# Moving a scale computation and a tile ahead in an attention and feed-forward block, and the place where its score banks change order

## What is computed

```
xn = layernorm(x)
s = attention(xn, Wq, Wk, Wv, Wo)      # 16 heads of 32, rope, causal softmax
h = gelu(bitlinear(xn, w_fc))          # 2048 hidden; ternary weights
g = silu(bitlinear(h, w_proj))
out = x + s * g
```

## Time and profile before

| | |
|---|---|
| median of 3 runs | 1154.88 us (1153.55 to 1155.67) |
| profiled execution, its own time | 1155.67 us |
| its span, first to last instruction | 1154.0 us |
| TensorE busy | 1108.0 us, 96% |
| VectorE busy | 856.8 us, 74% |
| ScalarE busy | 789.0 us, 68% |
| GpSimd busy | 506.0 us, 44% |

### The profile page before, as it was taken

How to read it: one execution, slowest core, us unless ns; L and a number is a source line. 1 busy time by engine, 2 the same in 40 slices (tenths; PEclk the granted TensorE clock), 3 DMA queues, 4 the chain that set the end, 5 groups by cost and what they waited for, 6 DMA issues and landing times.

```text
span 1154.0 us, 20237 instructions
## 1 busy us (share of the span) xinstructions
PE 1108.0 (96%) x7548; PEld 605.3 (52%) x7548; DVE 856.8 (74%) x1596; ACT 789.0 (68%) x1508; POOL 506.0 (44%) x915
## 2 busy tenths in 40 slices
PE   4989899999999999999999999999999999999997
PEld 3555654447444574446644475445844467444763
DVE  6987966788557885588756886579855888558864
ACT  4787884578835888179862788447882588727984
POOL 2035351473615626175342745146361553526433
PEclk9999999999999999999999999999999999999999
DMA  8491002730019101371016410183002910145111
GB/s 309 156 109 41 1 3 65 92 83 29 2 35 145 50 2 30 42 123 37 3 29 77 89 37 3 29 104 88 12 2 48 145 37 2 30 53 76 38 37 40
DMA packets 52610, 67.30 MB, mean 58 GB/s; under 512 B 9376, under 2 KB 34336, under 8 KB 52000
## 3 DMA queue, kind: packets, MB, share of 16 engines
q1 hardware_dynamic: 52512, 66.02, 30.0%
HBM read 31.98 MB, written 8.40 MB: 35 GB/s over the span
## 4 chain that ended last, share of the span: by engine, by line
PE 73%; DVE 7%; ACT 7%; POOL 6%; DMA 3%; issue 3%; SPq 1%; POOLq 0%; DVEq 0%; ACTq 0%
PE banks L421 20%; PE banks L547 18%; PE banks L592 11%; PE banks L526 5%; PE banks L673 4%; PE banks L438 4%; POOL arena L1374 4%; PE banks L603 3%; ACT banks L854 2%; ACT arena L877 2%; PE banks L654 2%; PE banks L533 2%; DVE mix L1142 2%; PE banks L452 1%; DMA stacks<-split_buf 1%
## 5 line engine op out<-in xcount | busy, mean ns | idle before, releaser
L854 ACT ACTIVATE banks<-banks,mix,scl 128x384 f32<-128x384 f32 (+2 forms) x384 | 248.6, 650 | 34.7 <-POOL mix L1351 32.0
L1142 DVE TENSOR_REDUCE mix<-banks 128x1 f32<-128x512 f32 (+3 forms) x352 | 215.5, 636 | 31.5 <-PE banks L533 27.3
L547 PE MATMUL banks<-xT,fcT 128*128 128x512 f16 x1024 | 227.9, 379 | 4.8 <-ACT xh_buf L818 4.7
L592 PE MATMUL banks<-proj_ones,arena 128*128 128x256 f16 (+1 forms) x1536 | 213.5, 273 | 0.3 <-DVE mix L1070 0.3
L1336 POOL TENSOR_TENSOR split_buf<-xr_buf,split_buf 128x512 f16<-128x512 f32 x64 | 74.6, 1186 | 314.2 <-ACT split_buf L795 314.2
L877 ACT ACTIVATE arena<-banks,scl 128x1280 f32<-128x1280 f32 x128 | 164.7, 1329 | 33.5 <-PE banks L654 29.3
L1342 POOL TENSOR_TENSOR xh_buf<-xh_buf 128x512 f32<-128x512 f32 x120 | 152.6, 1272 | 48.3 <-ACT xh_buf L818 42.0
L421 PE MATMUL banks<-xT,qkT 128*128 128x512 f16 x768 | 168.7, 379 | 0.0
L547 PEld LDWEIGHTS banks<-xT,fcT 128*128 128x128 f16 x1024 | 98.5, 98 | 124.3 <-ACT xh_buf L818 9.5
L592 PEld LDWEIGHTS banks<-proj_ones,arena 128*128 128x128 f16 x1536 | 141.3, 97 | 36.4 <-issue 0.6
L1351 POOL TENSOR_SCALAR mix<-mix,scl 128x1 f32<-128x1 f32 (+1 forms) x288 | 77.1, 268 | 182.2 <-DVE mix L1142 180.5
(11 more groups left out here) (163 smaller groups left out, 1469.2 us busy)
## 6 DMA issues: line engine op xcount, KB each, us to landing
stacks<-split_buf SPq DMA_DIRECT2D x192, 128.0 KB, 5.1
out_dram<-arena SPq DMA_DIRECT2D x32, 256.0 KB, 2.0
xr_buf<-in_L_attn_x_dram SPq DMA_DIRECT2D x7, 1024.0 KB, 6.9
resid<-in_L_attn_x_dram SPq DMA_DIRECT2D x28, 256.0 KB, 4.8
stacks<-in_L_ffn_w_fc_dram SPq DMA_DIRECT2D x1, 4096.0 KB, 25.9
arena<-in_L_ffn_w_proj_dram SPq DMA_DIRECT2D x1, 4096.0 KB, 14.8
mix<-norm_row SPq DMA_DIRECT2D x8, 256.0 KB, 4.9
xr_buf<-in_L_attn_x_dram SPq DMA_DIRECT2D x4, 256.0 KB, 3.8
```

The source lines that it names most:

```text
L547: mm = pe.matmul(banks[:, UP_BANKS[f % NUB], :], fcT[:, c, f * P:(f + 1) * P], xT[:, part, c, :], start=(c == 0 and part == 0), stop=(c == ...
L592: mm = pe.matmul(banks[:, DOWN_BANKS[h % 3], 0:cols.stop - cols.start], hid[:, part, f, t * P:(t + 1) * P], proj_ones[:, f, cols], start=( ...
L854: mm = nc.scalar.activation(block, block, ACT.Exp, scale=col(EXP_SCALE), bias=exp_bias[:, i, h0 + k:h0 + k + 1], accum_out=row_sum[:, i, h ...
L1142: nc.vector.tensor_reduce(row_max[:, i, h0:h0 + n], scores_of(r), AX_X, ALU.max).then_inc(max_ready, 1)
```

## The change

Four things are moved. The two rows of `S_BANKS` in which the order of banks changes stand at rounds 25 to 34 where they stood at rounds 15 to 24. VectorE scales tile 0 of the block before ahead of the up projection, after RoPE, and GpSimd adds its residual ahead of the squares' additions. VectorE makes `gate_scale` directly after centring, ahead of `finish_context(0)`. ScalarE's tanh no longer waits for `ffn_step`.

```
-S_BANKS = 3 * (3, 4, 0, 2, 1) + (3, 0, 4, 2, 1) + (0, 3, 2, 4, 1) + 4 * (0, 2, 3, 4, 1)
+S_BANKS = 5 * (3, 4, 0, 2, 1) + (3, 0, 4, 2, 1) + (0, 3, 2, 4, 1) + 2 * (0, 2, 3, 4, 1)
...
-OUT_SCALED_AFTER = 3
...
                     act.wait_ge(centred, b * NT + NT)
-                    act.wait_ge(ffn_step, b * 7 + 6)
                     nc.scalar.activation(tanh_sb[:, t, :], gate[:, t, :], ACT.Tanh,
...
+                if not first:
+                    scale_by_gate(b - 1, b * 8 + 8, range(OUT_EARLY))
+
                 def scores_of(r):
...
-                    if f == OUT_SCALED_AFTER and not first:
-                        scale_by_gate(b - 1, b * 8 + 8, range(OUT_EARLY))
...
                     centre(t, gate[:, t, :])
+                dve.wait_ge(rstd_ready, b + 1)
+                step(6, nc.vector.scalar_tensor_tensor(gate_scale[:, 0, :], rstd, col(HALF_GP), nan_if_0, ALU.mult, ALU.mult))
+                if not first:
+                    step(7, nc.vector.tensor_scalar(gate_scale[:, 1, :], gate_scale[:, 0, :], col(SVO), None, ALU.mult))
+
                 def finish_context(g):
...
-                    if g == 1:
-                        dve.wait_ge(rstd_ready, b + 1)
-                        step(6, nc.vector.scalar_tensor_tensor(gate_scale[:, 0, :], rstd, col(HALF_GP), nan_if_0, ALU.mult, ALU.mult))
-                        if not first:
-                            step(7, nc.vector.tensor_scalar(gate_scale[:, 1, :], gate_scale[:, 0, :], col(SVO), None, ALU.mult))
...
+                if not first:
+                    for t in range(OUT_EARLY):
+                        add_x(b - 1, t)
                 for f in range(1, FC):
...
-                    if f == OUT_SCALED_AFTER and not first:
-                        for t in range(OUT_EARLY):
-                            add_x(b - 1, t)
```

## The result

The changed kernel is slower: 1180.7 us median of 4 runs (1180.1 to 1181.3) against 1154.2 us for the kernel before, a ratio of 1.0228 with a 95% interval of 1.021 to 1.0246. That is 26.5 us more; 19.8 were forecast, with a range that ended at 1180. The direction, the two new stalls and the places without cost are as predicted. What took the time out of the range is a cost that the prediction did not have at all: 8.0 us in the profiled execution, some 6 in the timed ones.

The account below looks back on a forecast made before the run. TensorE, busy 96% of the span, was taken as the bound. Terms of 11.4 (early scale), 8.4 (bank order) and 0 (tile 0) sum to 19.8 us, making 1174.7 us from the 1154.88 median; range 1170 to 1180.

Parts of the forecast that it names:

- the two new stalls: TensorE waits at the heads' weighing for the context copy, 11.4 us, and in the score rounds for bank sums, 8.4 us.
- the places without cost: Tile 0's early scaling and residual add, and the tanh's dropped wait, were to cost and gain nothing.
- The bound: TensorE, busy 96% of the span; another engine's time costs nothing unless a matmul waits for it.
- Part 1, the stall: Heads' stage: early gate scale delays the context copy, so `weigh(2, 0)` starts 1.43 us late per middle block; 11.4 us in all.
- The choice of the shorter power: Masks and power on GpSimd take 1.75 us without `normalise` beside them; 11.4 us by this, 14.1 without.
- The step that failed: Behind `weigh(2, 0)` TensorE has no wait of 0.1 us or more until the up projection's, so the stall isn't absorbed.
- "more than the sum": `normalise` beside later masks, or residual add making squares miss slots, costs half to one us more a block; 1179 to 1184, chance 0.07.
- Part 2: Score rounds: new bank order makes round 30 wait 0.8 us and round 36 start 1.09 us late, not adding; 8.4 us.
- Part 3: Up projection: tile 0's earlier scaling and residual add cost 0, between -4.7 and +5 us; TensorE's 0.67 us wait stays.
- The rival on the other side: Moving tile 0's scale and residual removes the up projection's 0.67 us wait in seven blocks, -4.7 us; 1150.2, chance 0.03.
- The rivals of one part alone: Bank order free, only the early scale costs: 1166.3, chance 0.08; early scale free, only bank order costs: 1163.3, chance 0.04.

Follow-up runs that it names:

- `filled`: The changed kernel with ten extra matmuls of unused result on TensorE while it waits for group 0's context copy; 1174.3 us, ratio 1.0174.
- `after_rstd11`: The changed kernel with GpSimd making rstd behind the masks of head 11 instead of head 10; 1202.9 us, ratio 1.0423.
- `part3_tile0`: The kernel before with only tile 0's scaling and residual add moved ahead of the up projection; 1154.2 us, ratio 1.0001.
- `casts_apart`: The kernel before with ScalarE's two casts of RoPE's last pair split, behind the squares of chunks 0 and 1; 1149.9 us, ratio 0.9966.
- `part1_scale`: The kernel before with only the gate's scale made ahead of the contexts and the tanh's wait dropped; 1173.9 us, ratio 1.0168.
- `part2_banks`: The kernel before with only the order of the score banks changed; 1161.8 us, ratio 1.0069.

## Why the prediction was right and where it failed

- **The bound** is TensorE's order of work, as read; every cost found was a matmul that starts later or runs slower.
- **Part 1, the stall.** Right in mechanism, place and who waits. Predicted 11.4 us, 12.5 in the trace (1.56 a block instead of 1.43; the chain from mask to matmul takes 4.13 us and not 3.99). The choice of the shorter power was right: 1.04 us, with 0.77 for the masks, against 1.20 and 0.96 in the earlier trace rows. So the trace agrees with what the Trainium skill (GPSIMD Engine Reference, section 1) says of the interfaces that GpSimd shares with VectorE, by 0.16 us on the power. The masks of head 13, which now run beside `normalise`, took 1.17 us in place of 0.77.
- **The step that failed** is the sentence behind it, "behind 586.09 TensorE runs without a wait of 0.1 us or more up to the up projection's", taken as the reason that the stall is passed on at its own size. It took the matmuls behind the stall at the durations they had before it. They weren't: the clock fell to 1.2 GHz there in six of eight blocks, which is 8.0 of the profiled execution's 28.0 us, and 6.4 of the timed median's 26.5 by `filled`. `filled` shows the cause by taking it away with the stall left in place.
- The Trainium skill has such a loss of the clock as a rule (TensorE: Matmul & The Clock Gate, section "HAM oscillation — how this bites in real kernels"): a wait between short bursts of matmuls, once in every round of a loop, lowers the clock each time and its price is paid again each time. The waits there are given as 3 to 5 us. The trace agrees that the price is paid again, 1.4 to 1.6 us in five blocks and 0.3 in the first, but it was a wait of 2.0 us that did it, and in six blocks of eight; with 3.4 us (`after_rstd11`) it was all eight.
- **The rival "more than the sum"** gave 1179 to 1184, and the time lies there, but not by its mechanisms; that it does is luck. Its chance was 0.07, and no rival had the clock. The residual add costs nothing (`part3_tile0`, ratio 1.0001), and with `normalise` beside the same masks `filled` costs no more than the two stalls.
- **Part 2.** 8.4 us predicted, 8.1 in the trace and 8.0 by itself. Rounds 30 and 36 wait for the sums that were named, and they don't add. Three details were off. The first block pays 0.4 us and not 0.8. Round 36's wait was to show as 1.3 to 1.4 us and is 0.66, since TensorE comes to it 0.67 us late from round 30; its start is as computed. And round 32 is a new step of four too, behind 28, which the prediction's list leaves out; no wait shows there.
- **Part 3.** No cost and no gain, as said. The rival on the other side falls with it, and `casts_apart` shows that ScalarE's casts ahead of the square hold that wait.
- **The rivals of one part alone** fall: both parts cost by themselves, 20 and 8 us, and together 26.5.

## What to carry to other kernels

Where a change makes a TensorE-bound kernel's matmuls wait in the same place in every round of a loop, its price need not be the wait alone. Look for the granted clock behind the stall in the view by windows, and at the durations of the same matmuls before and after; where the clock is lower, add what it costs, here 1.4 to 1.6 us each time. When such a wait can't be removed, work of no use in it can be the cheaper way: here it gave back 6.4 us.

A wait put in an engine's queue holds up all that stands behind it. Here a wait and two tiny operations were moved ahead of a copy, and the copy was what TensorE needed. Ask, for each wait, which instruction of another engine is behind it, and by how much it was early.

## What was not expected of the hardware

A wait of 2.0 us (1.6 in the first block) in the heads' stage brought the granted clock from 2.4 to 1.2 GHz in some blocks and not in others, with the same instructions in the same order around it: in six of eight in the changed kernel (not in 3 and 6), and in six in `part1_scale` (not in 1 and 5). What decides between them was not tested, nor whether the same wait would do it where TensorE has more work around it. A wait of 3.4 us (3.0 in the first block, `after_rstd11`) did so in all eight, and the lower level lasted longer in four of them. Waits of 0.67 us twice a block, and of 1.5 us twice in the first block's score rounds, did not (`part2_banks`). Ten matmuls of 0.13 us each in the 2.0 us, with 0.72 us left idle, were enough to keep it up in all eight blocks.
